# Two-layer Mamba and mixture-of-experts network: softplus parts added on TensorE, five items read out by GpSimd in place of six, step rows stored ahead of the B and C rows

## What is computed

```python
dt = jax.nn.softplus(jnp.einsum('blr,dr->bld', dt, dt_proj_w) + dt_proj_b)
A = -jnp.exp(A_log)
def step(h, inputs):
    dt_t, B_t, C_t, u_t = inputs
    dA = jnp.exp(dt_t[:, :, None] * A)
    h = dA * h + (dt_t * u_t)[:, :, None] * B_t[:, None, :]
    y = jnp.einsum('bdn,bn->bd', h, C_t)
    return (h, y)
```

## Time and profile before

| | us |
|---|---|
| median of 3 runs | 1937.62 (1936.26 to 1938.16) |
| the profiled execution | 1938.45 |
| its span on the core | 1936.7 |
| VectorE busy | 1271.6 (66%) |
| GpSimd busy | 1211.5 (63%) |
| TensorE busy | 1546.9 (80%) |
| ScalarE busy | 991.2 (51%) |

### The profile page before, as it was taken

How to read it: one execution, slowest core, us unless ns; L and a number is a source line. 1 busy time by engine, 2 the same in 40 slices (tenths; PEclk the granted TensorE clock), 3 DMA queues, 4 the chain that set the end, 5 groups by cost and what they waited for, 6 DMA issues and landing times. The chain is left out here.

```text
span 1936.7 us, 25492 instructions
## 1 busy us (share of the span) xinstructions
PE 1546.9 (80%) x6220; PEld 927.2 (48%) x6221; DVE 1271.6 (66%) x2146; ACT 991.2 (51%) x1594; POOL 1211.5 (63%) x1179
## 2 busy tenths in 40 slices
PE   5677777777778998999982687777777777699996
PEld 3222222222228998989981222222222227566664
DVE  5799999999996531111115799999999996411012
ACT  4777777777772211222223777777777772122112
POOL 2699999999981001444435699999999992123310
PEclk8799999999995899999995799999999995599997
DMA  5788777787774204777765877788877881423313
GB/s 131 191 183 185 181 179 177 176 186 179 178 160 155 85 25 143 233 220 218 226 162 134 206 179 176 179 182 179 181 176 174 184 186 49 171 78 122 123 62 107
DMA packets 104507, 311.06 MB, mean 161 GB/s; under 512 B 19389, under 2 KB 74509, under 8 KB 93069
## 3 DMA queue, kind: packets, MB, share of 16 engines
q1 hardware_dynamic: 91896, 291.72, 60.1%
q0 software_dynamic: 12544, 18.63, 4.1%
HBM read 258.83 MB, written 51.45 MB: 160 GB/s over the span
## 5 line engine op out<-in xcount | busy, mean ns | idle before, releaser
L689 POOL TENSOR_TENSOR mamba_dbu<-mamba_rep 128x462 f32<-128x462 f32 x640 | 677.2, 1085 | 66.1 <-DMA mamba_rep<-dt_rows 66.1
L509 PE MATMUL mamba_ysum<-mamba_hc,all_sel 128*128 128x462 f32 x800 | 379.4, 588 | 148.3 <-DVE mamba_hc L797 147.3
L621 ACT ACTIVATE mamba_state<-mamba_rep,all_m_acol 128x462 f32<-128x462 f32 x640 | 388.9, 638 | 156.6 <-DVE mamba_last L808 155.6
L811 DVE TENSOR_TENSOR_SCAN mamba_state<-mamba_state,mamba_carry,mamba_dbu 128x462 f32<-128x462 f32 x400 | 455.4, 1179 | 0.0
L509 PEld LDWEIGHTS mamba_ysum<-mamba_hc,all_sel 128*128 128x128 f32 x800 | 130.3, 190 | 398.3 <-DVE mamba_hc L797 318.8
L808 DVE TENSOR_TENSOR_SCAN mamba_last<-mamba_state,mamba_last,mamba_dbu 128x462 f32<-128x462 f32 x240 | 280.3, 1168 | 15.2 <-POOL mamba_dbu L689 12.4
L684 POOL TENSOR_TENSOR mamba_hcp<-mamba_last,mamba_rep 128x462 f32<-128x462 f32 x240 | 266.7, 1111 | 5.6 <-DVE mamba_last L808 5.6
L504 PE MATMUL mamba_ysum<-mamba_hcp,all_sel 128*128 128x462 f32 x480 | 227.8, 570 | 50.1 <-POOL mamba_hcp L684 50.0
L797 DVE TENSOR_TENSOR mamba_hc<-mamba_state,mamba_rep 128x462 f32<-128x462 f32 (+1 forms) x240 | 230.7, 961 | 0.0
L1433 DVE TENSOR_TENSOR moe_h<-moe_sg,moe_up 128x512 f32<-128x512 f32 x62 | 42.6, 688 | 283.0 <-PE moe_up L1242 276.6
L504 PEld LDWEIGHTS mamba_ysum<-mamba_hcp,all_sel 128*128 128x128 f32 x480 | 85.3, 190 | 172.4 <-POOL mamba_hcp L684 119.6
(11 more groups left out here) (236 smaller groups left out, 2285.6 us busy)
## 6 DMA issues: line engine op xcount, KB each, us to landing
mamba_rep<-bc_rows SPq DMA_DIRECT2D x168, 462.0 KB, 7.4
mamba_rep<-dt_rows SPq DMA_DIRECT2D x168, 462.0 KB, 7.5
weights_wgu<-in_L_gu_dram SPq DMA_DIRECT2D x88, 512.0 KB
dt_rows<-mamba_dd SPq DMA_DIRECT2D x168, 115.5 KB, 7.2
weights_w<-in_L_w_dram SPq DMA_DIRECT2D x16, 1024.0 KB
mamba_xs<-seq_scratch SPq DMA_DIRECT2D x92, 116.0 KB, 9.2
seq_scratch<-mamba_y SPq DMA_DIRECT2D x40, 116.2 KB, 7.0
normed_rows<-xn SPq DMA_DIRECT2D x16, 288.0 KB, 7.1
```

The lines of the kernel that those rows point to most:

```text
L509: nc.tensor.matmul(ysum[:, 0:TC], sel[:, i // NM, :], hc[:, n % HCD, :], start=False, stop=end).then_inc(hc_summed, 1)
L621: nc.scalar.activation(state[:, STATE_BANK[i], 0:TC], rep[:, par * REP_ROWS + i // NM, :], ACT.Exp, scale=m["acol"][:, i:i + 1]).then_inc( ...
L689: pool.tensor_tensor(dbu[:, i % 4, :], rep[:, first + NG + i // NM, :], rep[:, first + 2 * NG + i % NM, :], ALU.mult).then_inc(dbu_ready, 1)
L811: nc.vector.tensor_tensor_scan(bank, bank, dbu[:, i % 4, :], carry[:, i:i + 1], ALU.mult, ALU.add).then_inc(scan_done, 1)
```

## The change

- `ON_POOL` has five items, 1, 4, 7, 10 and 13, in place of six. VectorE reads out eleven, five pairs and item 0 alone. A pair whose C rows don't lie side by side (11, 12) is read out in two instructions. `hc` has seven slots with a table of their order, `hcp` five.
- VectorE's `prep_ln` and `prep_dt` are gone. ScalarE writes the log to the tile `ab`; TensorE adds `ab`, `rx` and minus `rr` in PSUM by three products with the identity and the negated identity (`prep_add`) behind its eighth sum; ScalarE copies the result to `dd` behind item 15 (`prep_dd`).
- ScalarE's other work moves between the items: silu behind item 3 (was 6), exp behind 6 (was 10), the log behind 12 (was 15).
- TensorE's products for u and z are made one chunk earlier, behind the tenth sum; dt and B, C at the chunk's start. The sequence `xs` is loaded one chunk earlier too.
- GpSimd makes the step product for chunk k+1 behind the second dbu product of chunk k (was the fourth).
- SyncE issues `store_dt` first, then waits, then `replicate_bc`, `replicate_dt`, `store_bc` and `load_xs`. `dt_rows` has two halves, so that its address is computed per chunk.

```diff
-ON_POOL = (0, 3, 6, 8, 11, 13)
+ON_POOL = (1, 4, 7, 10, 13)
...
 SUM_ORDER = tuple(sorted(range(ITEMS), key=lambda i: LAST_OF[i] + 2 if i in ON_DVE else i + 3.1))
-HCP = 3
-HCD = 5
-
-
-AT_SILU, AT_EXP, AT_ONE, AT_LN, AT_BC, AT_DT, AT_DTU, AT_Y, AT_RR = 6, 10, 11, 15, 13, 3, 3, 2, 13
+HCP = 5
+HC_SLOT = (0, 1, 2, 3, 4, 5, 6, 1, 2, 3, 4)
+HC_GAP = tuple(min(d for d in range(1, ND + 1) if HC_SLOT[n - d] == HC_SLOT[n]) for n in range(ND))
+HCD = max(HC_SLOT) + 1
+
+
+AT_SILU, AT_EXP, AT_ONE, AT_BC, AT_LN, AT_U, AT_DTU, AT_Y, AT_RR, AT_ADD, AT_DD = 3, 6, 7, 8, 12, 9, 1, 2, 8, 7, 15
...
         half_ready, vare_ready, rstd_ready = sem("half_ready"), sem("vare_ready"), sem("rstd_ready")
-        MM_U, MM_Z, MM_DT, MM_BC, MMS = 1, 2, 3, 4, 4
-        A_U, A_Z, A_ABS, A_RELU, A_EXP, A_ONE, A_BC, A_LN, ACTS = 1, 2, 3, 4, 5, 6, 7, 8, 8
-        D_R, D_LR, D_DT, DVES = 1, 2, 3, 3
+        MM_U, MM_Z, MM_DT, MM_BC, MM_ADD, MMS = 1, 2, 3, 4, 5, 5
+        A_U, A_Z, A_ABS, A_RELU, A_EXP, A_ONE, A_BC, A_LN, A_DD, ACTS = 1, 2, 3, 4, 5, 6, 7, 8, 9, 9
+        D_R, DVES = 1, 1
...
                 sp.wait_ge(front_pool, START + k + 1)
+                half_rows = g["dt_rows"][bass.ds(half(k), 1), :, :]
                 for q in range(NG):
-                    rows = g["dt_rows"].rearrange("(d w q) n -> q d w n", w=2, q=NG)[q]
+                    rows = half_rows.rearrange("o (d w q) n -> q (o d) w n", w=2, q=NG)[q]
...
                 row = rep_row(k)
-                src = g["dt_rows"].rearrange("(d w) n -> d (w n)", d=DG)
+                src = g["dt_rows"][bass.ds(half(k), 1), :, :].rearrange("o (d w) n -> (o d) (w n)", d=DG)
...
                 sp.wait_ge(zeroed, 1)
-                for k in range(NCH, NCH + 3):
+                for k in range(NCH, NCH + 4):
...
             sp.wait_ge(seq_rest, 16 * RESTS)
+            sp.wait_ge(front_mm, START + MMS * 2 + MM_Z)
+            load_xs(3)
...
+                store_dt(k + 1)
                 sp.wait_ge(decay_ready, items_before)
...
                 replicate_bc(k + 1)
-                store_dt(k + 1)
                 replicate_dt(k + 1)
-                sp.wait_ge(front_mm, START + MMS * (k + 2) + MM_Z)
-                load_xs(k + 3)
                 store_bc(k + 2)
+                sp.wait_ge(front_mm, START + MMS * (k + 3) + MM_Z)
+                load_xs(k + 4)
...
             sp.wait_ge(bc_stored, 16 * (NCH + 2))
-            sp.wait_ge(xs_loaded, 32 * (NCH + 3))
+            sp.wait_ge(xs_loaded, 32 * (NCH + 4))
+            sp.wait_ge(dt_stored, 16 * NG * (NCH + 1))
             if l == 0:
...
             def prep_z(k):
+                pe.wait_ge(front_act, START + ACTS * k)
...
                                  start=True, stop=True).then_inc(front_mm, 1)
+
+            def prep_add(k):
+                pe.wait_ge(front_act, START + ACTS * k + A_LN)
+                nc.tensor.matmul(front[:, 1, 0:TC], g["ident"][:, :], ab[:, :], start=True, stop=False)
+                nc.tensor.matmul(front[:, 1, 0:TC], g["ident"][:, :], rx[:, :], start=False, stop=False)
+                pe.wait_ge(front_dve, START + DVES * k + D_R)
+                nc.tensor.matmul(front[:, 1, 0:TC], nident[:, :], rr[:, :], start=False, stop=True).then_inc(front_mm, 1)
...
                 if s == AT_U1:
+                    pe.wait_ge(minus_ready, 1)
+                    prep_add(0)
...
                 tiles["tensor_weights"](pe, 1)
+            prep_add(1)
+            prep_u(2)
+            prep_z(2)
             with pe.Fori(0, NCH) as k:
-                prep_u(k + 2)
-                prep_z(k + 2)
-
+                prep_dt(k + 2)
+                prep_bc(k + 2)
...
                         pe.wait_ge(hc_ready, START + ND * k + n + 1)
-                        nc.tensor.matmul(ysum[:, 0:TC], sel[:, i // NM, :], hc[:, n % HCD, :],
+                        nc.tensor.matmul(ysum[:, 0:TC], sel[:, i // NM, :], hc[:, HC_SLOT[n], :],
                                          start=False, stop=end).then_inc(hc_summed, 1)
-                    if at == AT_DT:
-                        prep_dt(k + 2)
-                    if at == AT_DT + 1:
-                        prep_bc(k + 2)
+                    if at == AT_ADD:
+                        prep_add(k + 2)
+                    if at == AT_U:
+                        prep_u(k + 3)
+                        prep_z(k + 3)
...
                 act.wait_ge(front_act, START + ACTS * k + A_BC)
-                nc.scalar.activation(front[:, 1, 0:TC], ex[:, :], ACT.Ln, bias=1.0).then_inc(front_act, 1)
+                nc.scalar.activation(ab[:, :], ex[:, :], ACT.Ln, bias=1.0).then_inc(front_act, 1)
+
+            def prep_dd(k):
+                act.wait_ge(front_mm, START + MMS * k + MM_ADD)
+                if not (isinstance(k, int) and k == 0):
+                    act.wait_ge(dt_stored, 16 * NG * k)
+                nc.scalar.activation(dd[:, 0, :], front[:, 1, 0:TC], ACT.Copy).then_inc(front_act, 1)
...
                 if s == AT_U1:
+                    prep_dd(0)
...
                     prep_rest(1)
+            prep_dd(1)
...
                                              scale=m["acol"][:, i:i + 1]).then_inc(decay_ready, 1)
+                        if i == AT_DD:
+                            prep_dd(k + 2)
...
-                pool.wait_ge(front_dve, START + DVES * k + D_DT)
+                pool.wait_ge(front_act, START + ACTS * k + A_DD)
...
-            def prep_ln(k):
-                dve.wait_ge(front_act, START + ACTS * k + A_LN)
-                dve.wait_ge(front_dve, START + DVES * k + D_R)
-                nc.vector.tensor_tensor(front[:, 1, 0:TC], front[:, 1, 0:TC], rr[:, :], ALU.subtract).then_inc(front_dve, 1)
-
-            def prep_dt(k):
-                if not (isinstance(k, int) and k == 0):
-                    dve.wait_ge(dt_stored, 16 * NG * k)
-                dve.wait_ge(front_dve, START + DVES * k + D_LR)
-                nc.vector.tensor_tensor(dd[:, 0, :], front[:, 1, 0:TC], rx[:, :], ALU.add).then_inc(front_dve, 1)
-
...
                     prep_rr(0)
-                    prep_ln(0)
-                    prep_dt(0)
...
             prep_rr(1)
-            prep_ln(1)
-            prep_dt(1)
...
                         nc.vector.tensor_copy(carry[:, i:end], state[:, bank:bank + width, TC - 1]).then_inc(carry_done, 1)
-                        dve.wait_ge(hc_summed, START + ND * k + n + width - HCD)
-                        nc.vector.tensor_tensor(hc[:, n % HCD:n % HCD + width, :], state[:, bank:bank + width, 0:TC],
-                                                rep[:, c_rows + i % NM:c_rows + i % NM + width, :], ALU.mult).then_inc(hc_ready, width)
+                        dve.wait_ge(hc_summed, START + ND * k + n + width - HC_GAP[n + width - 1])
+                        at_once = width if i % NM + width <= NM else 1
+                        for w in range(0, width, at_once):
+                            nc.vector.tensor_tensor(hc[:, HC_SLOT[n + w]:HC_SLOT[n + w] + at_once, :],
+                                                    state[:, bank + w:bank + w + at_once, 0:TC],
+                                                    rep[:, c_rows + (i + w) % NM:c_rows + (i + w) % NM + at_once, :], ALU.mult).then_inc(hc_ready, at_once)
...
                             read_out(i - 2 if SECOND[i - 1] else i - 1)
-                    prep_ln(k + 2)
                     read_out(ITEMS - 2 if SECOND[ITEMS - 1] else ITEMS - 1)
-                    prep_dt(k + 2)
...
                 ("wout", [P, DM]), ("vec", [P, 3]), ("diag", [P, DI]), ("acol", [P, ITEMS]))})
-        g["seq"] = nc.dram_tensor("seq_scratch", (NCH + 3, DM, CW), F32, kind="Internal").ap()
-        g["dt_rows"] = nc.dram_tensor("dt_rows", (2 * P, TC), F32, kind="Internal").ap()
+        g["seq"] = nc.dram_tensor("seq_scratch", (NCH + 4, DM, CW), F32, kind="Internal").ap()
+        g["dt_rows"] = nc.dram_tensor("dt_rows", (2, 2 * P, TC), F32, kind="Internal").ap()
```

More of the change, by code:

```diff
@@ L256, in phase_mamba @@
         u, sz = sb("u", [P, UBUFS, TC]), sb("sz", [P, UBUFS, TC])
+        nident = sb("nident", [P, P])
         ab, ex, rx, rr = sb("ab", [P, TC]), sb("ex", [P, TC]), sb("rx", [P, TC]), sb("rr", [P, TC])
@@ L277, in phase_mamba @@
         ysum, front = ps("ysum", [P, BANK]), ps("front", [P, 2, BANK])
-        xs_loaded, rep_loaded, bc_stored, dt_stored = sem("xs_loaded"), sem("rep_loaded"), sem("bc_stored"), sem("dt_stored")
+        xs_loaded, rep_loaded, bc_stored, dt_stored, minus_ready = sem("xs_loaded"), sem("rep_loaded"), sem("bc_stored"), sem("dt_stored"), sem("minus_ready")
         front_mm, front_act, front_dve, front_pool = sem("front_mm"), sem("front_act"), sem("front_dve"), sem("front_pool")
@@ L307, in phase_mamba @@
         LAG = 2 * GT - 1
-        RESTS = NCH - 3 + (3 if l == 0 else 0)
+        RESTS = NCH - 3 + (4 if l == 0 else 0)
         AT_W, AT_U0, AT_DT0, AT_U1, AT_DT1, AT_RR0, AT_DTU0 = ((7, 11, 14, 18, 20, 5, 19), (99, 11, 14, 18, 20, 5, 19))[l]
@@ L741, in _ @@
```

(2 more changed lines are left out.)

## The result

The changed kernel is slower: 2025.22 us median of 4 runs (2022.31 to 2029.55), against 1937.89 (1936.26 to 1940.13) for the kernel before measured beside it. The ratio is 1.045, with an interval from 1.043 to 1.0473. The profiled execution took 2022.31, span 2020.6, so 83.9 more span than before. L numbers of the changed kernel are its own; its scans are L828 and L831, the dbu products L719, the step product L679, the step stores L348, the B/C loads L355, the step loads L363.

What follows compares the result with a forecast made beforehand. VectorE and a DMA round trip nearly tie; the changed round trip decides: 3.2+0.15+3.05+0.6+19.3 = 26.3 us per chunk against 25.39, 36x0.91 = +32.8, plus 2 around the chunks, gives 1973 us, range 1944 to 2004.

Steps and rivals of the forecast that it cites:

- the last one: Round trip's last term, first B/C load issue to landing of all eight loads: 19.3 us, bounds 18.2 and 20.2.
- My first way: Estimate of the eight loads' time: the old 24.0 us less idle 1.9, stores' data 2.1 and xs loads 1.0, giving 19.0.
- The other terms: Rest of the round trip: products with signal 3.2, address step 0.15, four stores 3.05, way to first B/C load 0.6 us.
- Rival C: Round trip dearer: stores at 0.8 us each, loads at their upper bound; period 27.4, time 2012; chance 0.07.
- VectorE's floor: Shortest chunk period VectorE and ScalarE allow: VectorE's own work 24.4 us plus 0.4 waiting, 24.8.
- The wait at decay 4: VectorE waiting in mid-chunk for ScalarE's fourth decay, delayed by the silu block moved behind item 3: about 0.4 us.
- From landing to the first scan: At a chunk's start, GpSimd's first product and a signal, with no exp table load: 1.2 us in place of 2.15.
- TensorE's three products at nothing: Three added matrix products per chunk, 2.3 us on TensorE with 23% free: counted as nothing in the chunks.
- A: Rival: VectorE stays the bound, faster; period 24.8 and time 1919, or 1905 without the mid-chunk wait; chance 0.10.
- B: Rival: round trip at its low end, stores 2.55 us, loads landing in 18.4 to 19.1; time 1919 to 1941; chance 0.10.
- D: Rival: ScalarE's copy comes late, so GpSimd's step product waits for it and not for the landing; chance 0.02.
- Outside the chunks: Work around the chunk loop: +2 us on layer 0's first chunks, bounds 0 and +5; layer 1's covered by waits.

Runs made afterwards that it cites:

- e1: The changed kernel with the step stores put back behind the B/C loads in SyncE's order: 1938.06 us, ratio 1.0017 to the kernel before.
- e2: The kernel before with only SyncE's order changed, the step stores first: 2055.78 us, ratio 1.0627 to the kernel before.
- e3: The changed kernel with the step rows in one fixed place in DRAM, so no computed addresses: 1990.98 us, ratio 1.0286 to the kernel before.
- e4: The kernel before with step stores first and the step product behind the second dbu product, not the fourth: 1979.64 us, ratio 1.0248.
- e5: The changed kernel with GpSimd's step product made one chunk earlier, before the landing, stores still first: 1925.48 us, ratio 0.995 to the kernel before.

## Why the prediction was wrong, point by point

- **The direction and the mechanism held.** I gave slower 0.83, for the reason that the stores ahead of the B/C loads close the round trip. e1 and e2 show it from both sides: take the order back and the loss goes, add the order alone and it comes.
- **The size was too small: 1973 against 2025, and outside my range to 2004.** Counted from the profiled execution, 48.9 us are missing. The period was 27.44 on average and not 26.3, which is 36x1.14 = 41.0 of them; the first distances are 2.1, and what lies outside the chunks is 8.0 instead of 2, another 6.
- **The term that failed is the last one**, from the first bc issue to the landing of all eight loads: forecast 19.3, measured 20.13 (20.04 to 20.08 in e2, e3 and e4), so 0.83 of the missing 1.1. I took the data at the rates of two short windows, 224 and 217 GB/s, which gives 17.1, and 2.2 for start and receipt. The landings say what it is made of: the first load lands 4.4 behind its issue, and seven more follow at 2.245 each, 20.1 in all. The landings of the kernel before, 4.36 and seven times 2.19, would have given 19.7. So half of the 0.8 was there to be read, in landings instead of windows, and the other half is that a load takes 2.5% longer in the long piece. What slows it there I have not tested. My first way, to take the idle, the stores' data and the xs loads out of the 24.0 of before, gave 19.0 and was further off. It used one chunk's 24.0 where the median is 23.5, and took 1.0 out for xs loads that don't clear the way: in the changed kernel they go out at 227.12 and land about 4.0 later, together with the last step load. In e5, where they move only behind the last load's landing, the term is 19.98, which puts them at some 0.15 and not 1.0.
- **The other terms.** The two products, the step product with its signal and the address step: 3.35 forecast, 3.40 measured. The four stores: 3.05 forecast, 3.06 measured. The way from them to the first bc load: 0.6 forecast, 0.77 measured. Together 0.2 low. In e3 the fixed addresses gave these back as 3.19 and 3.36, so my 0.15 for the address step was right too (0.21).
- **Rival C is what happened.** Its period was 27.4 and the time 2012 (my upper bounds add up to 27.5, not 27.4). It put the long piece at the upper bound, which was right, and a store at 0.8, measured 0.76. I gave it only 0.07, although I had written down what spoke for it, that the loads had never run in one piece. With no row for the long piece, the upper bound should have been as likely as the middle. Even C's time misses by what lies outside the chunks.
- **VectorE's floor** of 24.8 came out by luck, and the changed kernel never reached it. e5 did, at 24.84. But its own work there is 24.65 a chunk and not 24.4: it fell by 0.35 from 25.00, not by 0.6. The wait at decay 4 is 0.18 instead of my 0.4, and the two errors cancel. Why the work fell by less than my sum says I have not looked into. In the changed kernel the wait at decay 4 is absent, since the first four decays run in a row at the landing (203.59 to 205.95), and VectorE stands idle 2.7 a chunk ((492.43-444.58)/18), where I had written 1.5.
- **From landing to the first scan** I had 1.2: 203.55 to 204.84 is 1.29. No table load stands there now. This is off the closed trip, which passes through GpSimd and not through VectorE.
- **TensorE's three products at nothing** held: e1 has them all and costs 0.17%, and its periods are shorter than before.
- **Rivals A, B and D** did not come. For D, the step product follows the second dbu product without idle. A would have needed a faster long piece.
- **The rate of the Trainium skill** (DMA: Bandwidth & Descriptors, section Bandwidth), 341 GB/s for 1 MB and more for larger sizes, is not what these runs show. Eight loads of 462 KB in a row ran at 211 GB/s by their landings, and four in a row at 216, so the longer piece was not faster. The page's rows are for one transfer of that size into 128 partitions, issued from GpSimd; here each load goes into 32 partitions and SyncE issues it, so it was no price for these.
- **Outside the chunks** I gave 2 us to the prologue of layer 0 (measured +0.7) and nothing to the rest. The stretch between the layers came out 4.4 longer; it scatters from 536.8 to 545.3 over all the kernels shown, so I lay no cause on it. Layer 1's first distance, 27.76 instead of 25.4, is not explained.

## What to carry to other kernels

When an issue is moved ahead of others on an in-order DMA queue, follow what it waits for back to the landing of the previous piece: if the circle closes, the period is the plain sum around it, however free every engine looks, and taking away SyncE's stall for the stores (380.1 to 386.3 before, 6 us) cost more than the stall did. Then look for the one operation that can be made before the landing; here moving one product of 1.1 us, with the order kept, turned +4.5% into -0.5%. And where a long piece of transfers has no row yet, take the time per load from the distance of landings and not from the GB/s of a window: here the window's rate gave 0.4 us too little, and the long piece was 0.4 dearer still, so the range should lean to the dear side.
